# Additive attention rows: the leaky sum in one ScalarE instruction, the mask added by VectorE

## The chip, the cores and the metric

The kernel runs on one core of a Trainium2 chip. The metric is the device time of one execution in microseconds; times of several executions are given as their median. A core has TensorE (PE; its weight loads are PEld), VectorE (DVE), ScalarE (ACT) and GpSimd (POOL), which run their own instruction streams and meet only at semaphores, and SyncE (SP), which here issues the DMAs.

## The reference

Four layers over a batch of 8 graphs with 2048 nodes and 64 features; after each, the input is added and a layer norm follows. Layer 0 is a gated neighbour sum. Layer 1 is dot-product attention with four heads and a second dot-product attention over their output. Layers 2 and 3 are attention with additive scores:

```
e   = left[:, :, None] + right[:, None, :]
e   = where(e >= 0, e, slope * e)            # slope 0.01 in layer 2, 0.2 in layer 3
att = softmax(where(mask, e, -inf))          # mask = adjacency; layer 2 also opens the diagonal
out = att @ h
```

## The kernel before, in words

The first 0.25 ms or so are layer 0 for all batches. The rest (`attention_layers`) is cut into rows: a row is 128 nodes of one attention unit against all 2048 nodes, so a unit has 16 rows. A batch has seven units: four heads (units 0 to 3), the second dot-product attention (unit 4, `GAT2`), and the two additive layers (unit 5, `ADD1`; unit 6, `ADD2`). The order of rows is written out by hand in `loop_order`: after a prologue come seven turns of a loop, and in each turn pairs of additive rows alternate with pairs of head rows of the next batch (first the 16 rows of `ADD1`, later the 16 of `ADD2`). In the last turn only three pairs of `ADD2` have head rows between them and the other ten rows follow each other. The epilogue has the last batch's unit 4, `ADD1` and `ADD2`, one unit after the other, with nothing between.

Every engine walks through the same steps, one row a step, in program order. For a dot-product row TensorE writes the scores of step s into `pss`, four banks of PSUM that hold one row. For an additive row ScalarE writes `pss` from SBUF (`lift_row`, L1283), a step ahead, in two halves. VectorE then reads each half (`masked_scores`, L1392), adds a second operand, takes the row's extremum and writes `rows`, a ring of four rows in SBUF. ScalarE takes the exponential in place (L1301). Two steps later TensorE turns the row in four tiles of 4 blocks (L1102) through `ring`, three banks of PSUM; a tile is copied to `pt` by ScalarE (L1253) or VectorE (L1404): of a dot-product row two tiles each, of an additive row one by ScalarE and three by VectorE. Then TensorE multiplies by the values (`po`, L1129), a pair of rows at a time.

The second operand of L1392 is the mask (bf16, SBUF) for a dot-product row. For an additive row it is a row that GpSimd has put into `rows` beforehand (`mask_row`): slope times the right terms (`sr`) plus the mask (L925), and in `ADD2` also a 128x128 block `shut` that closes the diagonal where the adjacency has no self edge (L922, L929). What ScalarE lifts is the rest of the leaky sum, a ReLU with scale (1-slope)/slope. GpSimd makes the masked row one step ahead, as soon as the ring's place is free.

Beside the rows each engine has tasks hung on steps. VectorE's that matter here: `bend_block` (L1411, leaky ReLU of 256 columns of `zt`, in place), the low halves of projections (L1355, two instructions), the layer norms (L1375, L317, L319, L326, L328). GpSimd's: scaling finished pairs (`finish`, L938 to L951) and the layer norms' powers and products (L894 to L908). The projection tile `hc` is turned by TensorE at L1061, the input of an additive layer at L1032.

Of the kernel before, what the change touches and what calls it, by code (L numbers as in the profile page):

```python
# [34 lines left out]
P = 128  # L35
# [645 lines left out]
def attention_layers(nc, x1, out, whd, bh, wod, bo, gamma, beta, w2, a2, w3, a3,  # L681
# [3 lines left out]
    with ctx:  # L685
# [22 lines left out]
        shut = sb("shut", [P, P], BF16)  # L708
# [47 lines left out]
        mr_ready = sem("mr_ready")  # L756
# [119 lines left out]
        def _(pool):  # L876
# [4 lines left out]
            sr_c = Count(sr_ready)  # L881
            tr_c = Count(tr_ready)
            mr_c = Count(mr_ready)
# [4 lines left out]
            def run_task(name, unit, c):  # L888
# [18 lines left out]
                elif name in ("ld", "rb"):  # L907
                    nc.gpsimd.tensor_tensor(xbc, xbc, spread(rstd, CH), ALU.mult)\  # L908
                      .then_inc(x_done if unit == ADD2 else x_ready, 1)
                elif name == "r":  # L910
                    sr_c.n += 1
# [3 lines left out]

            def mask_row(row):

                if row.t == 0:
                    wait(sr_c)
                if row.unit == ADD2:  # L920
                    drain_link(pool)
                    nc.gpsimd.tensor_tensor(shut[:], ident[:], shut_by[:, row.t:row.t + 1].to_broadcast([P, P]),  # L922
                                            ALU.mult)
                wait(tr_c, tr_c.n + NC * (row.slot_user + 1))
                masked = nc.gpsimd.tensor_tensor(rows[:, row.slot, :], sr[:], mask[:, row.t, :], ALU.add)  # L925
                if row.unit == ADD2:
                    drain_link(pool)
                    own = rows[:, row.slot, row.t * P:(row.t + 1) * P]
                    masked = nc.gpsimd.tensor_tensor(own, own, shut[:], ALU.add)  # L929
                masked.then_inc(mr_ready, 1)  # L930
# [23 lines left out]
            def run_segment(segment):  # L954
                for s in segment.steps:
                    row = segment.row(s + 1)
                    if row and not row.gat and row.t > 0:
                        mask_row(row)
# [4 lines left out]

                    if row and not row.gat and row.t == 0:
                        mask_row(row)
                copied_c.n += segment.pairs
                rc_c.n += segment.pairs
                tr_c.n += NC * segment.blocks
                mr_c.n += segment.adds
# [204 lines left out]
        def _(act):  # L1174
# [28 lines left out]
            def run_task(name, unit, c):  # L1203
# [26 lines left out]
                elif name == "h":  # L1230
# [3 lines left out]
                    nc.scalar.mul(ls[:, unit - ADD1, blocks].unsqueeze(2), pair[:, :, D:D + 1], 1.0 - SLOPES[unit])  # L1234
                    nc.scalar.copy(rt[:, blocks].unsqueeze(2), pair[:, :, D + 1:D + 2]).then_inc(lr_ready, 1)
                    nc.scalar.copy(hn[hn_of(unit)][:, blocks, :], pair[:, :, 0:D]).then_inc(hn_ready, 1)
                elif name == "r":
                    next_of(right_c)
                    sr_c.n += 1
                    nc.scalar.mul(sr[:, cols], px[:], SLOPES[unit]).then_inc(sr_ready, 1)  # L1240
# [33 lines left out]
            def lift_row(row, half):  # L1274

                slope = SLOPES[row.unit]
# [237 lines left out]
```

## Time and profile before

| | |
|---|---|
| median of three runs | 5698.53 us (5693.42 to 5699.99) |
| the profiled execution | 5694.06 us, span of the trace 5692.3 us |
| mean granted TensorE clock | 0.973 of full |
| busy: TensorE / VectorE / ScalarE / GpSimd | 93% / 78% / 65% / 34% of the span |
| instructions of the span | 131823 |

Busy shares are means over stretches of different kinds; a turn of the loop takes about 666 us, of which the two stretches with additive rows take about 166 and 176 us.

### The profile page before, as it was taken

Reading aid. Unit: us, or ns where it says so; the run is one execution under the profiler, and the core shown is the slowest. Engines: PE = TensorE matmul, PEld = TensorE weight load, DVE = VectorE, ACT = ScalarE, POOL = GpSimd, SP = SyncE. Lnnn points to the kernel's source line nnn. Section 1 sums busy time; section 2 is a strip of 40 time slices with the busy share of each in tenths; the row PEclk is TensorE's granted clock in tenths of the full one; section 3 lists DMA queues with packets and bytes.
Section 4 is the critical chain, followed back from the end, with each engine's and each line's share of the span. In section 5 each row is a group of like instructions: output and inputs, shape, how many; then the busy total and the mean of one; then the engine's idle time right before and its main releaser. Section 6 shows DMA issues by size and latency. Waiting matters only on the chain.

```text
span 5692.3 us, 131823 instructions
## 1 busy us (share of the span) xinstructions
PE 5277.2 (93%) x52866; PEld 4523.5 (79%) x52866; DVE 4418.0 (78%) x7321; ACT 3722.7 (65%) x5489; POOL 1940.8 (34%) x1724
## 2 busy tenths in 40 slices
PE   8499999999999899999999999998999999999866
PEld 6388888878878788787888888787887878888755
DVE  5677678787787778877787877877788777877766
ACT  3266567675676757776576766767577766767665
POOL 4300024251243413333242522425133332424366
PEclk9799999999999999999999999999999999999988
DMA  5200000000000000000000000000000000000000
GB/s 177 61 16 11 18 9 9 9 11 18 9 13 7 13 14 13 13 7 15 15 9 9 11 18 9 13 5 14 15 13 12 7 15 14 9 9 5 13 1 5
DMA packets 135486, 94.35 MB, mean 17 GB/s; under 512 B 93792, under 2 KB 112864, under 8 KB 134880
## 3 DMA queue, kind: packets, MB, share of 16 engines
q1 hardware_dynamic: 134880, 85.92, 6.0%
q8 instruction: 423, 6.93, 0.5%
q14 instruction: 183, 1.50, 0.1%
HBM read 35.03 MB, written 8.91 MB: 8 GB/s over the span
## 4 chain that ended last, share of the span: by engine, by line
PE 75%; DVE 8%; issue 5%; ACT 4%; DVEq 2%; POOLq 1%; DMA 0%; SPq 0%; POOL 0%; ACTq 0%
PE po L1129 24%; PE ring L1102 24%; PE pss L1093 10%; PE pss L1094 10%; DVE rows L1392 3%; DVE pt L1404 3%; PE ring L1051 2%; ACT rows L1301 2%; PE ring L1117 2%; DVEq L311 2%; POOLq L311 1%; ACT pss L1283 1%; PE ring L1068 1%; DVE ha L1355 1%; PE ring L1061 1%
## 5 line engine op out<-in xcount | busy, mean ns | idle before, releaser
L1102 PE MATMUL ring<-ident,rows 128*128 128x128 f32 x14336 | 1942.0, 278 | 137.3 <-DVE pt L1404 85.0
L1301 ACT ACTIVATE rows<-rows,nm 128x2048 f32<-128x2048 f32 x896 | 1794.6, 2003 | 315.3 <-DVE nm L1392 310.4
L1404 DVE COPY pt<-ring 128x512 f32<-128x512 f32 x2048 | 1330.4, 685 | 840.4 <-PE ring L1102 834.0
L1102 PEld LDWEIGHTS ring<-ident,rows 128*128 128x128 f32 x14336 | 1606.1, 142 | 373.5 <-issue 204.5
L1129 PE MATMUL po<-pt,hn 128*64 128x128 f32 x28672 | 1776.8, 277 | 35.0 <-ACT zt L1260 22.5
L1129 PEld LDWEIGHTS po<-pt,hn 128*64 128x64 f32 x28672 | 1562.6, 138 | 190.2 <-issue 166.8
L1253 ACT COPY pt<-ring 128x512 f32<-128x512 f32 x1536 | 837.2, 588 | 771.8 <-PE ring L1102 761.5
L925 POOL TENSOR_TENSOR rows<-sr,mask 128x2048 f32<-128x2048 f32 x256 | 1052.2, 4112 | 416.9 <-PE ring L1102 410.6
L1093 PE MATMUL pss<-ha 128*128 128x512 f32 x2560 | 1068.7, 417 | 39.3 <-DMA ha<-hb 38.1
L1094 PE MATMUL pss<-ha,hb 128*128 128x512 f32 x2560 | 1015.1, 397 | 0.0
L1392 DVE CUSTOM_DVE_ANT_0 rows<-pss,mask,nm 128x1024 f32<-128x1024 f32 x640 | 821.5, 1284 | 89.3 <-issue 3.4
L1392 DVE CUSTOM_DVE_ANT_0 rows<-pss,mask 128x1024 f32<-128x1024 f32 x640 | 772.8, 1208 | 86.4 <-PE pss L1094 48.5
L938 POOL TENSOR_TENSOR zt<-zt,ob 128x128 f32<-128x128 f32 x256 | 117.5, 459 | 1786.0 <-ACT ob L1271 1786.0
L1283 ACT ACTIVATE pss<-sr,ls 128x1024 f32<-128x1024 f32 x512 | 563.6, 1120 | 71.5 <-DVE nm L1392 69.5
L1093 PEld LDWEIGHTS pss<-ha 128*128 128x128 f32 x2560 | 486.4, 190 | 127.6 <-DMA ha<-hb 40.5
L1094 PEld LDWEIGHTS pss<-ha,hb 128*128 128x128 f32 x2560 | 487.6, 190 | 86.9
L1392 DVE CUSTOM_DVE_ANT_0 rows<-pss,rows,nm 128x1024 f32<-128x1024 f32 x256 | 328.6, 1284 | 34.8 <-issue 1.0
L894 POOL TENSOR_TENSOR st<-st,half_power 128x4 f32<-128x4 f32 x128 | 131.6, 1028 | 656.4 <-DVE st L330 656.4
L1392 DVE CUSTOM_DVE_ANT_0 rows<-pss,rows 128x1024 f32<-128x1024 f32 x256 | 305.2, 1192 | 38.9 <-POOL rows L929 23.6
L1423 DVE RECIPROCAL rcw<-rs 128x128 f32<-128x128 f32 x256 | 241.5, 943 | 1.2
L940 POOL TENSOR_SCALAR zt<-zt,bhs 128x128 f32<-128x128 f32 x256 | 154.8, 605 | 44.0 <-issue 44.0
L1219 ACT COPY hc<-ring 128x512 f32<-128x512 f32 x80 | 46.9, 586 | 185.7 <-PE ring L1051 185.7
(109 smaller groups left out, 3291.2 us busy)
## 6 DMA issues: line engine op xcount, KB each, us to landing
hb<-ha SPq DMA_DIRECT2D x160, 128.0 KB, 2.3
ha<-hb SPq DMA_DIRECT2D x160, 128.0 KB, 2.3
adjb<-in_adj SPq DMA_DIRECT2D x32, 512.0 KB, 5.5
xb<-in_x SPq DMA_DIRECT2D x16, 256.0 KB, 2.9
x<-t SPq DMA_DIRECT2D x16, 256.0 KB, 2.4
xin<-x SPq DMA_DIRECT2D x32, 128.0 KB, 2.5
xb<-x SPq DMA_DIRECT2D x8, 512.0 KB, 3.9
out<-xb SPq DMA_DIRECT2D x32, 128.0 KB, 2.1
```

What stands on the lines that cost most here:

```text
L311: eng.drain()
L925: masked = nc.gpsimd.tensor_tensor(rows[:, row.slot, :], sr[:], mask[:, row.t, :], ALU.add)
L1093: nc.tensor.matmul(pss[:, cols], ha[i][:, rows_t], moving, start=True, stop=False)
L1094: last = nc.tensor.matmul(pss[:, cols], hb[i][:, rows_t], moving, start=False, stop=True)
L1102: last = nc.tensor.transpose(tile[:, r * P:(r + 1) * P], rows[:, row.slot, jb * P:(jb + 1) * P], ident[:])
L1129: last = nc.tensor.matmul(po[side * D:(side + 1) * D, 0:P], hn[row.hn][:, r, :], pt[:, r, first + side, :], start=(r == 0), stop=(r == NB ...
L1253: nc.scalar.copy(pt[:, CH * q:CH * (q + 1), row.k % SLOTS, :], tile_of("turn", row.k, q)[:].rearrange("p (j n) -> p j n", n=P)).then_inc(p ...
L1283: nc.scalar.activation(pss[:, cols], sr[:, cols], ACT.Relu, scale=(1.0 - slope) / slope, bias=ls[:, row.unit - ADD1, row.t:row.t + 1]).the ...
L1301: nc.scalar.activation(rows[:, row.slot, :], rows[:, row.slot, :], ACT.Exp, scale=-1.0, bias=nm[:, row.place, 1:2], accum_out=rs[:, row.pl ...
L1392: nc.vector.tensor_tensor_reduce(out=scores, in0=pss[:, cols], in1=mask[:, row.t, cols] if row.gat else scores, scale=-1.0, scalar=(-2 * M ...
L1404: nc.vector.tensor_copy(pt[:, CH * q:CH * (q + 1), row.k % SLOTS, :], tile_of("turn", row.k, q)[:].rearrange("p (j n) -> p j n", n=P)).the ...
L1423: nc.vector.reciprocal(rcw[:].rearrange("p (r n) -> p r n", r=2), rs[:, pair].unsqueeze(2).to_broadcast([P, 2, D])).then_inc(rc_ready, 1)
```

## The change

ScalarE's `lift_row` becomes one parametric ReLU with the slope as its `alpha`, on right term plus left bias, so that `pss` holds the whole leaky sum; the small copies of left and right terms lose their factors. `masked_scores` adds the mask itself for every kind of row. For an `ADD2` row VectorE first adds the diagonal block into `pss` in a `scalar_tensor_tensor` of 128 columns in the half where the block lies. GpSimd's `mask_row`, its tile `shut` and the semaphore `mr_ready` go away; VectorE waits in its place for the ring's place to be free, as dot-product rows do.

```diff
@@ gpsimd
-            def mask_row(row):
-                if row.t == 0:
-                    wait(sr_c)
-                if row.unit == ADD2:
-                    drain_link(pool)
-                    nc.gpsimd.tensor_tensor(shut[:], ident[:], shut_by[:, row.t:row.t + 1].to_broadcast([P, P]),
-                                            ALU.mult)
-                wait(tr_c, tr_c.n + NC * (row.slot_user + 1))
-                masked = nc.gpsimd.tensor_tensor(rows[:, row.slot, :], sr[:], mask[:, row.t, :], ALU.add)
-                if row.unit == ADD2:
-                    drain_link(pool)
-                    own = rows[:, row.slot, row.t * P:(row.t + 1) * P]
-                    masked = nc.gpsimd.tensor_tensor(own, own, shut[:], ALU.add)
-                masked.then_inc(mr_ready, 1)
@@ scalar, tasks "h" and "r"
-                    nc.scalar.mul(ls[:, unit - ADD1, blocks].unsqueeze(2), pair[:, :, D:D + 1], 1.0 - SLOPES[unit])
+                    nc.scalar.copy(ls[:, unit - ADD1, blocks].unsqueeze(2), pair[:, :, D:D + 1])
-                    nc.scalar.mul(sr[:, cols], px[:], SLOPES[unit]).then_inc(sr_ready, 1)
+                    nc.scalar.copy(sr[:, cols], px[:]).then_inc(sr_ready, 1)
@@ scalar, lift_row
-                nc.scalar.activation(pss[:, cols], sr[:, cols], ACT.Relu, scale=(1.0 - slope) / slope,
-                                     bias=ls[:, row.unit - ADD1, row.t:row.t + 1]).then_inc(lift_ready, 1)
+                nc.scalar.activation(pss[:, cols], sr[:, cols], ACT.Prelu, scale=1.0,
+                                     bias=ls[:, row.unit - ADD1, row.t:row.t + 1],
+                                     alpha=SLOPES[row.unit]).then_inc(lift_ready, 1)
@@ vector, masked_scores
                 if half == 0:
-                    if not row.gat:
-                        wait(mr_c, mr_c.n + row.nth + 1)
-                    elif row.slot_user >= 0 or tr_c.n:
+                    if row.slot_user >= 0 or tr_c.n:
                         wait(tr_c, tr_c.n + NC * (row.slot_user + 1))
                 else:
                     drain_link(dve)
                 count = scores_c if row.gat else lift_c
                 wait(count, count.n + 2 * row.nth + half + 1)
+                if row.unit == ADD2 and row.t * P // HALF == half:
+                    own = pss[:, row.t * P:(row.t + 1) * P]
+                    nc.vector.scalar_tensor_tensor(out=own, in0=ident[:], scalar=shut_by[:, row.t:row.t + 1],
+                                                   in1=own, op0=ALU.mult, op1=ALU.add)
+                    drain_link(dve)
                 nc.vector.tensor_tensor_reduce(
-                    out=scores, in0=pss[:, cols], in1=mask[:, row.t, cols] if row.gat else scores,
+                    out=scores, in0=pss[:, cols], in1=mask[:, row.t, cols],
```

## Rows read from the trace of the kernel before

**Rows 1.** The page: busy us and share of each engine, instructions.
```profile
PE 5277.2 (93%) x52866; PEld 4523.5 (79%) x52866; DVE 4418.0 (78%) x7321; ACT 3722.7 (65%) x5489; POOL 1940.8 (34%) x1724
```

**Rows 2.** First turn's additive stretches: us, PE, PEld, DVE, ACT, POOL busy; clock.
```profile
887.00:1053.00 166.00, 153.97 (x1629) 130.80 (x1627) 145.02 (x234) 130.01 (x182) 75.91 (x44) 0.98 0.05 11
...
1144.00:1320.00 176.00, 160.52 (x1691) 137.20 (x1691) 142.56 (x233) 130.31 (x182) 88.22 (x72) 0.97 0.05 12
```

**Rows 3.** Groups of instructions, GpSimd: count, busy us, mean ns, idle before.
```profile
L925 POOL TENSOR_TENSOR rows<-sr,mask 128x2048 f32<-128x2048 f32 x256 | 1052.2, 4112 | 416.9 <-PE ring L1102 410.6 <-ACT sr L1240 6.1
```

**Rows 4.** VectorE: two groups with their means; three lines with min/median/max ns.
```profile
L1411 DVE SCALAR_TENSOR_TENSOR zt<-zt 128x256 f32<-128x256 f32 x128 | 105.2, 822 | 0.0
L1355 DVE TENSOR_TENSOR ha<-hc,hb 64x512 fp32r<-64x512 f32 x80 | 79.8, 997 | 1.1
...
L1411 DVE SCALAR_TENSOR_TENSOR zt<-zt x128: 411/421/2864, 323.0 to 5286.6; 128x256 f32<-128x256 f32 x128
...
L1355 DVE TENSOR_TENSOR ha<-hc,hb x80: 689/690/4458, 253.0 to 5305.7; 64x512 fp32r<-64x512 f32 x80
...
L319 DVE SCALAR_TENSOR_TENSOR xb<-st,xb x96: 424/425/4053, 775.6 to 5686.5; 128x256 f32<-128x256 f32 x96
```

**Rows 5.** Timeline near 1015 us: start, duration, engine, line.
```profile
1015.26 4.40 POOL L925 TENSOR_TENSOR rows<-sr,mask 128x2048 f32<-128x2048 f32 x1 [0.41 <-PE ring L1102]
1015.75 4.46 DVE L1355 TENSOR_TENSOR ha<-hc,hb 64x512 fp32r<-64x512 f32 x1
...
1020.98 1.12 PE L1061 MATMUL ring<-ident,hc 128*128 128x128 f32 x4 [5.81 <-DVE pt L1404]
1021.89 1.91 PE L1102 MATMUL ring<-ident,rows 128*128 128x128 f32 x8
```

**Rows 6.** Timeline near 1274 us, VectorE and TensorE.
```profile
1273.78 2.46 DVE L1411 SCALAR_TENSOR_TENSOR zt<-zt 128x256 f32<-128x256 f32 x1
...
1276.89 1.33 PE L1051 MATMUL ring<-zt,wo 64*64 64x128 f32 x10 [2.32 <-DVE pt L1404]
```

**Rows 7.** Durations by line, min/median/max ns: the lift, a table load, additive L1392.
```profile
L1283 ACT ACTIVATE pss<-sr,ls x512: 1097/1119/1162, 883.1 to 5659.3; 128x1024 f32<-128x1024 f32 x171
...
L580 ACT ACT_TABLE_LOAD  x1: 1283/1283/1283, 0.7 to 0.7; - x1
...
L1392 DVE CUSTOM_DVE_ANT_0 rows<-pss,rows x256: 1152/1212/1227, 887.2 to 5661.7; 128x1024 f32<-128x1024 f32 x128
L1392 DVE CUSTOM_DVE_ANT_0 rows<-pss,rows,nm x256: 1282/1284/1286, 888.5 to 5663.1; 128x1024 f32<-128x1024 f32 x128
```

**Rows 8.** Timeline of a mixed `ADD2` pair in the first turn.
```profile
1166.43 2.17 PE L1102 MATMUL ring<-ident,rows 128*128 128x128 f32 x16
...
1167.19 1.29 DVE L1404 COPY pt<-ring 128x512 f32<-128x512 f32 x2
...
1171.57 1.29 DVE L1404 COPY pt<-ring 128x512 f32<-128x512 f32 x2 [0.53 <-PE ring L1102]
```

**Rows 9.** Timeline of the epilogue: `ADD1` starts and runs, then `ADD2` starts.
```profile
5449.81 2.15 ACT L1283 ACTIVATE pss<-sr,ls 128x1024 f32<-128x1024 f32 x2
...
5453.89 1.22 DVE L1392 CUSTOM_DVE_ANT_0 rows<-pss,rows 128x1024 f32<-128x1024 f32 x1 [12.03 <-POOL rows L925]
...
5455.26 1.28 DVE L1392 CUSTOM_DVE_ANT_0 rows<-pss,rows,nm 128x1024 f32<-128x1024 f32 x1
...
5466.34 1.21 DVE L1392 CUSTOM_DVE_ANT_0 rows<-pss,rows 128x1024 f32<-128x1024 f32 x1
...
5470.69 1.22 DVE L1392 CUSTOM_DVE_ANT_0 rows<-pss,rows 128x1024 f32<-128x1024 f32 x1
...
5573.55 2.15 ACT L1283 ACTIVATE pss<-sr,ls 128x1024 f32<-128x1024 f32 x2
...
5578.65 1.22 DVE L1392 CUSTOM_DVE_ANT_0 rows<-pss,rows 128x1024 f32<-128x1024 f32 x1 [13.04 <-POOL rows L929]
...
5583.81 1.23 DVE L1392 CUSTOM_DVE_ANT_0 rows<-pss,rows 128x1024 f32<-128x1024 f32 x1 [2.50 <-POOL rows L929]
```

More of the change, by code:

```diff
@@ L707, in attention_layers @@
         ob = sb("ob", [P, 2, D], F32)
-        shut = sb("shut", [P, P], BF16)
         nm = sb("nm", [P, NB, 2], F32)
@@ L755, in attention_layers @@
         lift_ready = sem("lift_ready")
-        mr_ready = sem("mr_ready")
         scores_read = sem("scores_read")
@@ L880, in _ @@
             rc_c = Count(rc_ready)
-            sr_c = Count(sr_ready)
-            tr_c = Count(tr_ready)
-            mr_c = Count(mr_ready)
             def wait(count, n=None):
@@ L909, in run_task @@
                       .then_inc(x_done if unit == ADD2 else x_ready, 1)
-                elif name == "r":
-                    sr_c.n += 1
             def each(v):
                 return v[:].unsqueeze(1).to_broadcast([P, CH, D])
-            def mask_row(row):
-                if row.t == 0:
-                    wait(sr_c)
-                if row.unit == ADD2:
-                    drain_link(pool)
-                    nc.gpsimd.tensor_tensor(shut[:], ident[:], shut_by[:, row.t:row.t + 1].to_broadcast([P, P]),
-                                            ALU.mult)
-                wait(tr_c, tr_c.n + NC * (row.slot_user + 1))
-                masked = nc.gpsimd.tensor_tensor(rows[:, row.slot, :], sr[:], mask[:, row.t, :], ALU.add)
-                if row.unit == ADD2:
-                    drain_link(pool)
-                    own = rows[:, row.slot, row.t * P:(row.t + 1) * P]
-                    masked = nc.gpsimd.tensor_tensor(own, own, shut[:], ALU.add)
-                masked.then_inc(mr_ready, 1)
             def finish(row):
@@ L955, in run_segment @@
                 for s in segment.steps:
-                    row = segment.row(s + 1)
-                    if row and not row.gat and row.t > 0:
-                        mask_row(row)
                     if segment.finished(s):
@@ L962, in run_segment @@
                         run_task(*task)
-                    if row and not row.gat and row.t == 0:
-                        mask_row(row)
                 copied_c.n += segment.pairs
                 rc_c.n += segment.pairs
-                tr_c.n += NC * segment.blocks
-                mr_c.n += segment.adds
             run_segments(run_segment)
@@ L1274, in lift_row @@
             def lift_row(row, half):
-                slope = SLOPES[row.unit]
                 cols = slice(half * HALF, (half + 1) * HALF)
@@ L1326, in _ @@
             lift_c = Count(lift_ready)
-            mr_c = Count(mr_ready)
             tr_c = Count(tr_ready)
@@ L1449, in run_segment @@
                 lift_c.n += 2 * segment.adds
-                mr_c.n += segment.adds
                 drain_link(dve)
```

## The prediction

> **What bounds the kernel now.** I read the page first: TensorE is busy 93% of the span and VectorE 78% [rows 1], and the chain that ended last is made of TensorE's matmuls for the most part. So TensorE is the bound, and a change that touches only the other three engines can move the time only where TensorE stands still. Next I read the stretches. Where additive rows alternate with head rows, TensorE is idle 12.0 of 166 us (`ADD1`) and 15.5 of 176 us (`ADD2`), with VectorE busy 87% and 81% and GpSimd 46% and 50% [rows 2]. That is where the changed work lies, seven times over. The groups show what GpSimd does there: 256 instructions of 4.1 us, 1052 us in all [rows 3]. The table of waits has almost no wait of VectorE for them in the loop, so at first sight they cost nothing.
>
> The durations by line say otherwise. L1411 takes 421 ns in the median and 2864 at most; L1355 690 and up to 4458; L319 425 and up to 4053 [rows 4]. All have two inputs in SBUF. The timeline shows where the long ones lie: an L1355 of 4.46 us began 0.49 us after an L925 and ended at 1020.21, 0.55 us after that L925 (1019.66) [rows 5]. VectorE was counted as busy, but was held for the length of GpSimd's instruction. L1392 with one input in PSUM never shows this (1282 to 1286 ns in 256 instructions, half of all additive halves) [rows 7]. What the reader is to see in [rows 5, 6] is who pays: VectorE's copy of a turned tile stands behind the held instruction, the bank of `ring` comes free late, and TensorE waits 5.81 and 2.32 us.
>
> **The change part by part.**
>
> *The masked rows go (gain in the loop).* Held time is mean less median, times the count: L1411 128 x (822 - 421) = 51.3 us, L1355 80 x (997 - 690) = 24.6 us, together 76 us [rows 4]. All of L1411 and L1355 lies ahead of the epilogue's additive rows. The other form of L1355 is held a little too; I set it against the few that end behind GpSimd's short instructions, which stay. How much of it does TensorE feel? L1411 held for 2.04 us (2.46 - 0.42) gave a wait of 2.32 us, and L1355 held for 3.77 us, with an L1411 shortly before, one of 5.81 us [rows 5, 6]. TensorE waits for such copies now and then where nothing is held, so some of it would be waited anyway. I take 0.9: 68 us. The bounds are 0.5 and 1.
>
> After the wait of 5.81 us TensorE's clock is low: 8 transposes took 1.91 us, where 16 take 2.17 us at full clock, and the four ahead of them 1.12 us against 0.54 by the same rate [rows 5, 8]. So the wait costs another 0.83 + 0.58 = 1.4 us. It comes once in each of the seven turns, and less than 1 us of wait should be left in its place, as after the shorter waits, which show no slow matmul: 7 x 1.4 = 10 us. Bounds 0 and 10.
>
> The page SBUF — State Buffer of the Trainium skill (section Who interferes with whom) has the mechanism as a rule: a VectorE instruction with two SBUF inputs and a GpSimd instruction that reads SBUF exclude each other for a whole instruction, and with at most one SBUF input VectorE is not held. The trace agrees, with 4.46 us against 0.69 us. By the rule the new block instruction, with `ident` in SBUF and `pss` in PSUM, would not be held either; no row here shows that form.
>
> *The diagonal block moves to VectorE (cost).* 128 new instructions of 128 columns. From L1411's 411 ns at 256 columns and L1392's 1212 ns at 1024, a column costs 1.04 ns, which gives 411 - 133 = 278 ns. A per-partition scalar adds at most what `nm` adds to L1392, 1284 - 1212 = 72 ns, so 0.28 to 0.35 us [rows 4, 7]. The drain before the next instruction costs 0.15 us, as between the halves of L1392 (the first ends at 5455.11, the second begins at 5455.26) [rows 9]. I take 0.47 us each, with bounds 0.28 and 0.6. That is 60 us of VectorE in all. In a mixed pair the first of them stands ahead of the copies at 1167.19. TensorE turned four tiles from 1166.43 in 2.17 us with three banks: the fourth began about 1168.0, and the first copy ended about 1167.8 [rows 8]. So there is 0.2 us of slack, and 0.47 us late makes TensorE 0.3 us late here. The second adds another 0.47 us, but there VectorE waited 0.53 us for TensorE anyway [rows 8], and it waits again in the two head rows behind. Other pairs carry VectorE tasks as well, so I take 0.4 us a pair. Six turns have 8 mixed pairs, the last one 3: 51 x 0.4 = 20 us. Bounds 0, and 51 x 0.94 = 48 us.
>
> *The lift (no cost).* Same instruction, operands and columns: 1119 ns, with a spread of 65 ns [rows 7]. What the function and its `alpha` add is not in the trace. ScalarE ran copies, ReLUs, squares and exponentials after one single table load, so functions shared a table. I take 0; below nothing is excluded by the same columns, above stands the rival below. The copies without a factor are the same ScalarE instructions; 0.
>
> *The wait.* VectorE now waits for the ring's place where it waited for GpSimd. GpSimd waited for the same turns first and then took 4.1 us, so the new wait ends earlier in all cases. Queued behind it are the other half, the copies and tasks.
>
> *Epilogue (gain).* `ADD1` began its first L1392 4.08 us after its lift began, held by L925; with the first half lifted in 1.1 us it can begin 2.9 us sooner. For `ADD2` the distance is 5.10 us against 1.1 + 0.47, so 3.5 us [rows 9]. Then `ADD2` ran a row in 5.16 us, each waiting for GpSimd (5583.81 less 5578.65), and `ADD1` in 4.35 us on VectorE (5470.69 less 5466.34) [rows 9]. With the block that is 4.82, so 0.34 us a row over 15 rows, 5 us. One L319 was held 3.6 us there [rows 4]; I give 3 of it. In all 14 us, bounds 8 and 20. The ten rows at the end of the last turn run at GpSimd's pace too: 8 x 0.34 = 3 us.
>
> *Sum* against the profiled execution of 5694.06 us: -68 - 10 + 20 - 14 - 3 = -75, so 5619. The median of the runs shown is 4.5 us above that execution; for a median I forecast 5623 us.
>
> **The rivals.**
>
> *VectorE takes back more.* VectorE is busy 87% in the first mixed stretch as it is [rows 2], and the order of rows is tight. If every block instruction passes whole (48 us in the loop) and only half of the held time was felt (38 us, no clock gain), the sum is -38 + 48 - 17 = -7; with one of the two alone it is -47 (-68 - 10 + 48 - 17) or -35 (-38 + 20 - 17). With both it would be no change that can be told; the case stands for one of them. For it: 0.2 us of slack in [rows 8]. Against it: VectorE waits for TensorE several times in each group of four rows. Time 5650 to 5685.
>
> *Slower: the parametric ReLU is in another table than the exponential.* Place: between L1283 and L1301 on ScalarE. Each additive row would need two loads, 256 x 2 x 1.283 = 657 us of ScalarE [rows 7]. ScalarE is idle 36 of 166 us in the mixed stretch [rows 2], and 32 loads there are 41 us, so it would become the bound, and most loads lie ahead of an exponential that TensorE waits for. At half of them felt: 5623 + 330 = 5950. It decides once more than 75 of the 657 us pass. Against it: the single load of the trace, though that covers only the functions used. The page ScalarE: Activation LUTs of the Trainium skill (section Table sets: the hidden batching unit) says that cheap functions are in every set, but does not list this one, and puts a switch at about 2.66 us with its drain; by that figure the 512 would be an estimated 1360 us. The trace has 1.283 us for the load alone.
>
> *Not felt.* The held instructions cost VectorE time that it would have waited for TensorE anyway, and the gains of the epilogue are eaten by the block: within 11 us of before. Against it stand the two waits of TensorE in [rows 5, 6].
>
> **How the numbers follow.** Forecast (5592 to 5650): 0.68. VectorE takes back more (5650 to 5687): 0.17. More than I count, from GpSimd's other work coming sooner and waits that vanish whole (below 5592; with every bound on its good side -76 - 10 - 0 - 20 - 3 = -109, 5590): 0.06. Not felt: 0.04. Another table: 0.05. What a measurement of this kernel can tell from no change is about 0.2%, 11 us. Faster 0.68 + 0.17 + 0.06 = 0.91, same 0.04, slower 0.05. The range 5592 to 5668 leaves out 0.06 below, and above it 0.09 and about a quarter of the second case, 0.2 in all.
>
> **What the profile after would show.** Right: L1411 and L1355 with maxima below 1 us; TensorE's wait near 1021 us below 1 us and no slow transposes after it; the first mixed stretch some 8 us shorter than 166, the second about even (4 us less held, 3 more of block); L1283 at 1.12 us and one table load; 128 new VectorE instructions of about 0.33 us; the epilogue's first `ADD1` scores 1.2 us after the lift begins; `ADD2` rows at 4.8 us. Wrong: held instructions still there behind L894 to L951; TensorE's waits for L1404 in the `ADD2` stretch growing by more than 0.5 us a pair; table loads between lift and exponential.

## The result and the profile after

The changed kernel takes 5621.3 us in the median of four runs (5620.65 to 5622.09), the kernel before 5698.6 us (5693.42 to 5699.99): a ratio of 0.9866 with a 95% interval of 0.9849 to 0.9883, so 77 us less. The forecast was 5623 us with a range of 5592 to 5668.

The page of the profile after, first the busy time and instructions of each engine, then of its groups those that answer to [rows 1] and to the two waits that matter below (busy us, mean ns, idle time before and its releaser):

```profile
PE 5261.1 (94%) x52866; PEld 4501.0 (80%) x52866; DVE 4372.5 (78%) x7449; ACT 3722.1 (66%) x5489; POOL 775.2 (14%) x1212
...
L1071 PE MATMUL ring<-ident,rows 128*128 128x128 f32 x14336 | 1939.5, 278 | 114.6 <-DVE pt L1375 79.9
...
L1098 PE MATMUL po<-pt,hn 128*64 128x128 f32 x28672 | 1770.9, 276 | 45.3 <-ACT zt L1229 32.5
```

GpSimd has lost 1166 us of busy time. In the loop that alone gives nothing, as VectorE hardly ever waited for it there; it did in the epilogue [rows 9]. VectorE has 45 us less, although it got 128 instructions more and no old one was made cheaper. Its two held lines show why; the view is the durations by line (min/median/max ns), to be read against [rows 4]. L1382 is the old L1411, L1323 the old L1355:

```profile
L1382 DVE SCALAR_TENSOR_TENSOR zt<-zt x128: 411/416/424, 324.3 to 5231.5; 128x256 f32<-128x256 f32 x128
...
L1323 DVE TENSOR_TENSOR ha<-hc,hb x80: 687/689/795, 253.9 to 5246.9; 64x512 fp32r<-64x512 f32 x80
...
L1360 DVE SCALAR_TENSOR_TENSOR pss<-ident,shut_by,pss x128: 271/354/358, 1138.1 to 5590.8; 128x128 f32<-128x128 f32 x128
...
L1251 ACT ACTIVATE pss<-sr,ls x512: 1094/1119/1163, 884.4 to 5587.2; 128x1024 f32<-128x1024 f32 x171
...
L319 DVE SCALAR_TENSOR_TENSOR xb<-st,xb x96: 424/425/427, 776.9 to 5614.5; 128x256 f32<-128x256 f32 x96
...
L580 ACT ACT_TABLE_LOAD  x1: 1283/1283/1283, 0.7 to 0.7; - x1
```

The medians stood still and the maxima fell from 2864, 4458 and 4053 ns to 424, 795 and 427. The lift has the same 1119 ns as a parametric ReLU as it had as a ReLU [rows 7], and there is one table load, so the parametric ReLU needed no load of its own beside the exponential. The block instruction takes 336 ns in the mean.

The place of [rows 5], in the timeline after:

```profile
1014.87 0.69 DVE L1323 TENSOR_TENSOR ha<-hc,hb 64x512 fp32r<-64x512 f32 x1
1015.59 1.29 DVE L1375 COPY pt<-ring 128x512 f32<-128x512 f32 x2
...
1016.34 0.66 PE L1030 MATMUL ring<-ident,hc 128*128 128x128 f32 x4 [0.99 <-DVE pt L1375]
1017.02 1.06 PE L1071 MATMUL ring<-ident,rows 128*128 128x128 f32 x8
```

The low halves take 0.69 us in place of 4.46, TensorE waits 0.99 us in place of 5.81, and the 8 transposes behind it take 1.06 us in place of 1.91. In the stretches of the first turn (us, then PE, PEld, DVE, ACT, POOL busy, clock), which answer to [rows 2]:

```profile
888.50:1047.60 159.10, 152.81 (x1629) 129.73 (x1629) 138.85 (x236) 129.78 (x181) 15.54 (x29) 1.00 0.05 12
1138.50:1313.80 175.30, 160.38 (x1695) 135.47 (x1695) 143.89 (x250) 130.94 (x182) 15.48 (x29) 0.98 0.05 12
```

The first has 7 us less, of them 5.7 us of TensorE's idle time and 1.2 us of its busy time (the slow matmuls); its clock rose from 0.98 to 1.00. The second hardly moved. I measured all stretches of both traces in the same way, from where VectorE starts on the scores of a stretch's first additive row to where it starts on those of the first row behind its last. In the epilogue, too, a unit's part ends with the first scores of the next: how late `ADD1` starts counts to unit 4, and how late `ADD2` starts counts to `ADD1`. In us, summed over the seven turns:

| | before | after | difference |
|---|---|---|---|
| `ADD1` among head rows | 1169.0 | 1114.4 | -54.6 |
| between the two | 633.2 | 636.2 | +3.0 |
| `ADD2` among head rows | 1228.1 | 1220.1 | -8.0 |
| epilogue: unit 4, `ADD1`, `ADD2` | 140.8, 124.8, 113.6 | 137.7, 117.7, 110.6 | -13.2 |

The differences sum to 72.8 us; the two profiled executions, 5694.06 and 5622.09 us, are 72 us apart, the medians 77. Of the 54.6 us, 39.8 are idle time of TensorE and 14.8 its busy time, that is slower matmuls, in all seven turns: the first turn with its 1.2 us has one of the smallest parts.

The epilogue, against [rows 9] (start, duration, engine, line):

```profile
5390.72 2.15 ACT L1251 ACTIVATE pss<-sr,ls 128x1024 f32<-128x1024 f32 x2
...
5391.98 1.23 DVE L1363 CUSTOM_DVE_ANT_0 rows<-pss,mask 128x1024 f32<-128x1024 f32 x1 [9.19 <-ACT pss L1251]
...
5508.02 2.15 ACT L1251 ACTIVATE pss<-sr,ls 128x1024 f32<-128x1024 f32 x2
...
5509.24 0.35 DVE L1360 SCALAR_TENSOR_TENSOR pss<-ident,shut_by,pss 128x128 f32<-128x128 f32 x1 [9.15 <-ACT pss L1251]
5509.71 1.22 DVE L1363 CUSTOM_DVE_ANT_0 rows<-pss,mask 128x1024 f32<-128x1024 f32 x1
...
5517.11 1.22 DVE L1363 CUSTOM_DVE_ANT_0 rows<-pss,mask 128x1024 f32<-128x1024 f32 x1
```

`ADD1` scores 1.26 us after its lift begins, where it took 4.08 us, and `ADD2` 1.69 us where it took 5.10. VectorE's wait there is now for ScalarE.

What is still open is whether the held time is the cause of the gain, what the block costs, and why its gain in `ADD2` is so small. The experiments ask that.

### The profile page after: what moved, and what is told of

It reads as the page before. It is cut to its first block, busy times and chain, and to the rows that moved or that the text cites. A ratio compares the mean times of both kernels' runs of the same rounds, so it can differ in the third digit from the quotient of the medians.

```text
span 5620.3 us, 131303 instructions
## 1 busy us (share of the span) xinstructions
PE 5261.1 (94%) x52866; PEld 4501.0 (80%) x52866; DVE 4372.5 (78%) x7449; ACT 3722.1 (66%) x5489; POOL 775.2 (14%) x1212
## 4 chain that ended last, share of the span: by engine, by line
PE 76%; DVE 8%; issue 5%; ACT 4%; DVEq 2%; DMA 0%; SPq 0%; POOLq 0%; POOL 0%; ACTq 0%
PE po L1098 24%; PE ring L1071 24%; PE pss L1062 10%; PE pss L1063 10%; DVE rows L1363 4%; DVE pt L1375 3%; PE ring L1020 2%; DVEq L311 2%; ACT rows L1270 2%; PE ring L1086 2%; ACT pss L1251 1%; PE ring L1037 1%; ACT pt L1222 1%; PE ring L1030 1%; PE ring L1001 1%
## 5 line engine op out<-in xcount | busy, mean ns | idle before, releaser
L1363 DVE CUSTOM_DVE_ANT_0 rows<-pss,mask,nm 128x1024 f32<-128x1024 f32 x896 | 1150.2, 1284 | 124.1 <-issue 5.8
L1363 DVE CUSTOM_DVE_ANT_0 rows<-pss,mask 128x1024 f32<-128x1024 f32 x896 | 1079.8, 1205 | 105.3 <-PE pss L1063 48.8
L1394 DVE RECIPROCAL rcw<-rs 128x128 f32<-128x128 f32 x256 | 241.6, 944 | 1.2
L924 POOL TENSOR_TENSOR y<-ob,rc 128x128 f32<-128x128 f32 x128 | 51.3, 401 | 1225.1 <-ACT ob L1240 1180.5
L1270 ACT ACTIVATION_READ_ACCUMULATOR rows<-rows,nm 128x1 f32 x896 | 167.8, 187 | 0.0
L1363 DVE DVE_READ_ACCUMULATOR2_ANT nm<- 128x1 f32 x1792 | 148.5, 83 | 0.0
```

Of the source, the lines that this page charges most:

```text
L1270: nc.scalar.activation(rows[:, row.slot, :], rows[:, row.slot, :], ACT.Exp, scale=-1.0, bias=nm[:, row.place, 1:2], accum_out=rs[:, row.pl ...
L1363: nc.vector.tensor_tensor_reduce(out=scores, in0=pss[:, cols], in1=mask[:, row.t, cols], scale=-1.0, scalar=(-2 * MASKED if half == 0 else ...
L1394: nc.vector.reciprocal(rcw[:].rearrange("p (r n) -> p r n", r=2), rs[:, pair].unsqueeze(2).to_broadcast([P, 2, D])).then_inc(rc_ready, 1)
```

## Experiments

Every run was measured against the kernel before on the same chip (medians from 5697.4 to 5699.7 us). "Over the changed kernel" means over 5621.3 us.

### What does the diagonal block cost? noblock and block2

noblock leaves out the closing of `ADD2`'s diagonal (the output lacks just that):

```diff
-                if row.unit == ADD2 and row.t * P // HALF == half:
-                    own = pss[:, row.t * P:(row.t + 1) * P]
-                    nc.vector.scalar_tensor_tensor(out=own, in0=ident[:], scalar=shut_by[:, row.t:row.t + 1],
-                                                   in1=own, op0=ALU.mult, op1=ALU.add)
-                    drain_link(dve)
```

> The kernel after, but the diagonal block instruction of ADD2 (128 of them, VectorE) and its drain are left out, so ADD2's diagonal is not closed where the adjacency has no self edge. Theory of the prediction: 0.4 us a mixed pair x 51 pairs = 20 us in the loop, and up to 0.49 us a row in the 26 additive rows that follow each other (13 us, of which 8 felt): 5621 - 28 = 5593 us (5585 to 5603). Rival 1, every block instruction passes whole: 128 x 0.49 = 63 us, so 5558. Rival 2, all of it hidden in VectorE's waits: 5621 within 4.

Measured: 5599.1 us (5595.1 to 5602.7), ratio 0.9829 (0.9814 to 0.9843). The block costs 22 us. `ADD2`'s seven stretches sum to 1201.9 us without it, 1220.1 with it; of these 18.2 us, 11.5 are idle time of TensorE and 6.6 slower matmuls.

block2 issues the block and its drain twice:

```diff
+                    for _ in range(2):
                         nc.vector.scalar_tensor_tensor(out=own, in0=ident[:], ...)
                         drain_link(dve)
```

> The block instruction and its wait for the pipeline are issued twice at each of the 128 rows of ADD2 that need it (the second adds the shut value to the diagonal once more, so the value is -2 times as low; the output changes by nothing that matters, the diagonal weights are zero either way). Theory A (a pair's cycle in ADD2's mixed stretches passes through VectorE, so the time given to it comes back at about the measured rate of 22 us per block): about 5645, 5640 to 5652, ADD2's mixed stretches 178 to 180. Theory B (the first block eats slack left by the removed hold, the second finds none, so it costs its full 0.35 to 0.47 us x 112 in the loop and x 16 in the epilogue): 5660 to 5680. Theory C (most of the first block's price is its wait for ScalarE's lift, which the second doesn't pay): under 5635.

Measured: 5658.8 us (5654.3 to 5661.4), ratio 0.9932 (0.9915 to 0.9949). The second block costs 37.5 us, 15 more than the first and more than theory A gave; the time lies just short of theory B's interval. `ADD2`'s stretches go to 1247.6 us (+27.5), the epilogue's `ADD2` from 110.6 to 115.8 us. The timeline shows the mechanism. This is a mixed `ADD2` pair of the first turn, in the changed kernel (start, duration, engine, line, and in brackets the idle time before and its releaser):

```profile
1207.64 0.68 DVE L1323 TENSOR_TENSOR hb<-hc,ha 64x512 fp32r<-64x512 f32 x1
1208.02 1.09 PE L1071 MATMUL ring<-ident,rows 128*128 128x128 f32 x8
1208.33 0.69 DVE L1323 TENSOR_TENSOR ha<-hc,hb 64x512 fp32r<-64x512 f32 x1
...
1209.05 1.29 DVE L1375 COPY pt<-ring 128x512 f32<-128x512 f32 x2
...
1209.89 0.83 PE L1071 MATMUL ring<-ident,rows 128*128 128x128 f32 x5 [0.34 <-DVE pt L1375]
```

and the same place in block2:

```profile
1206.28 1.09 PE L1071 MATMUL ring<-ident,rows 128*128 128x128 f32 x8
...
1207.74 1.29 DVE L1376 COPY pt<-ring 128x512 f32<-128x512 f32 x2
...
1208.58 0.94 PE L1071 MATMUL ring<-ident,rows 128*128 128x128 f32 x6 [0.77 <-DVE pt L1376]
```

In noblock TensorE does not stand here, but its matmuls just before were slow (32 in 3.30 us, for 1.97 in the changed kernel), which gave the copies time. The next such place has the same speed in both. The changed kernel waits there, noblock doesn't:

```profile
1233.71 1.16 PE L1071 MATMUL ring<-ident,rows 128*128 128x128 f32 x8 [0.34 <-DVE pt L1375]
```

```profile
1233.97 1.16 PE L1071 MATMUL ring<-ident,rows 128*128 128x128 f32 x8
```

With one block TensorE waits 0.34 us (0.27 and 0.25 us at the like places at 1163 and 1255), with two 0.77 us. So one block with its drain, about 0.47 us, finds some 0.13 us of slack and passes on 0.34; the second finds none and passes on 0.43. That is the step of the prediction that set 0.2 us of slack against 0.47.

### Is it the reading that holds VectorE? ghost, ghostset, ghostlong

These put work back on GpSimd that nobody reads, for the same rows and behind the same waits, into a part of a tile that is not in use. ghost:

```diff
+                wait(tr_c, tr_c.n + NC * (row.slot_user + 1))
+                drain_link(pool)
+                nc.gpsimd.tensor_tensor(by_block(xz[D:P, BANK:N]), ident[D:P, :].unsqueeze(1).to_broadcast([D, 12, P]),
+                                        by_block(mask[D:P, row.t, BANK:N]), ALU.add)
+                drain_link(pool)
```

> The kernel after, with a GpSimd instruction that nobody waits for put back at each additive row, at the step and behind the wait of the old masked row: it adds ident (repeated) and 1536 columns of the mask on 64 partitions into an unused part of xz. An estimate from 4.1 us at 2048 columns is 3.1 us each. Theory A (a GpSimd instruction that reads SBUF and a VectorE instruction with two SBUF inputs exclude each other): held instructions come back with maxima of 3 to 3.5 us, three quarters of the 69 us of the two mixed stretches are lost again: 5621 + 45 to 60 = 5666 to 5681; the starts of ADD1 and ADD2 in the epilogue stay fast. Theory B (the gain came from VectorE and the ring no longer waiting for GpSimd's row): no change against after, 5621 within 5.

Measured: 5629.8 us (5627.6 to 5634.2), 8.5 us over the changed kernel. Both theories' numbers were missed: the instruction was shorter than L925 (3.12 us against 4.11), and so its end fell ahead of the low halves. The timeline near the place of [rows 5]:

```profile
1013.51 3.12 POOL L914 TENSOR_TENSOR xz<-ident,mask 64x1536 f32<-64x1536 f32 x1 [0.16 <-issue]
...
1015.66 0.69 DVE L1390 COPY pt<-ring 128x512 f32<-128x512 f32 x1
1016.26 0.66 DVE L1397 SCALAR_TENSOR_TENSOR zt<-zt 128x256 f32<-128x256 f32 x1
1016.85 0.67 DVE L1338 TENSOR_TENSOR hb<-hc,ha 64x512 fp32r<-64x512 f32 x1
```

The bend began at 1016.26 and ended at 1016.92, 0.29 us behind the end of GpSimd's at 1016.63; the low half behind it was free. In the loop only the bends were held (mean 531 ns, maximum 1141: 14 us in all), and in the epilogue one L319 (3172 ns).

ghostset does the same with instructions that only write:

```diff
+                for _ in range(3):
+                    drain_link(pool)
+                    nc.gpsimd.memset(xz[D:P, BANK:N], 0.0)
+                drain_link(pool)
```

> As ghost, but GpSimd writes SBUF without reading it: three memsets of 1536 columns on 64 partitions at each additive row, an estimated 1.5 us each. Theory A with the rule that only GpSimd's reads collide: nothing held beyond after, 5621 within 5. Theory A in a wider form (any use of SBUF by GpSimd excludes): holds of up to 1.5 us, 5621 + 15 to 40. Theory B: 5621 within 5.

Measured: 5623.6 us (5620.4 to 5627.9), 2.3 us over the changed kernel, whose runs (5620.65 to 5622.09) lie within its own. GpSimd is as busy with them (768 x 1.374 = 1055 us) as with L925 before (1052 us), and no line of VectorE is held:

```profile
L915 POOL MEMSET xz<- x768: 1372/1374/1391, 877.5 to 5584.7; 64x1536 f32 x192
...
L1397 DVE SCALAR_TENSOR_TENSOR zt<-zt x128: 411/417/423, 320.6 to 5230.5; 128x256 f32<-128x256 f32 x128
...
L1338 DVE TENSOR_TENSOR ha<-hc,hb x80: 687/689/799, 250.5 to 5245.9; 64x512 fp32r<-64x512 f32 x80
```

This isn't for want of meetings: 66 bends and 28 low halves began while a memset ran, and none of them took more than 422 and 691 ns. In the kernel before, each of the 42 bends that began during an L925 took 808 ns or more. So it isn't GpSimd's being busy. To have ghost's read at L925's length, ghostlong reads the first input with a stride:

```diff
-                nc.gpsimd.tensor_tensor(by_block(xz[D:P, BANK:N]), ident[D:P, :].unsqueeze(1).to_broadcast([D, 12, P]),
-                                        by_block(mask[D:P, row.t, BANK:N]), ALU.add)
+                nc.gpsimd.tensor_tensor(xz[D:P, BANK:N].rearrange("p (q n) -> p q n", n=32),
+                                        ident[D:P, 0:P:4].unsqueeze(1).to_broadcast([D, 48, 32]),
+                                        mask[D:P, row.t, BANK:N].rearrange("p (q n) -> p q n", n=32), ALU.add)
```

> As ghost, but the first input is read with a stride of 4 elements, which should make GpSimd's instruction longer than the 3.12 us that missed most of VectorE's two-input instructions (in ghost one ended 0.2 us before L1355 began). I guess 4 to 4.8 us. Theory A: the holds come back, as long as GpSimd's instruction lasts, and the time goes up by 0.5 (as in ghost: 8.5 us for 17.5 us held) to 0.9 of the held time: with 30 to 70 us held, 5640 to 5675. Theory B: 5621 to 5632.

Measured: 5700.7 us (5696.9 to 5705.9), ratio 1.0003 (0.9994 to 1.0012). The whole gain is gone, by an instruction whose result nobody waits for. The durations by line, and then the timeline of one turn:

```profile
L914 POOL TENSOR_TENSOR xz<-ident,mask x256: 3776/3906/4231, 884.0 to 5667.1; 64x1536 f32<-64x1536 f32 x128
...
L1398 DVE SCALAR_TENSOR_TENSOR zt<-zt x128: 412/421/1949, 327.1 to 5310.3; 128x256 f32<-128x256 f32 x128
...
L1339 DVE TENSOR_TENSOR ha<-hc,hb x80: 689/689/4198, 256.6 to 5325.7; 64x512 fp32r<-64x512 f32 x80
...
L1376 DVE SCALAR_TENSOR_TENSOR pss<-ident,shut_by,pss x128: 272/354/358, 1148.8 to 5674.4; 128x128 f32<-128x128 f32 x128
```

```profile
1016.15 3.94 POOL L914 TENSOR_TENSOR xz<-ident,mask 64x1536 f32<-64x1536 f32 x1 [0.16 <-issue]
...
1018.90 1.48 DVE L1398 SCALAR_TENSOR_TENSOR zt<-zt 128x256 f32<-128x256 f32 x1
...
1020.57 4.05 POOL L914 TENSOR_TENSOR xz<-ident,mask 64x1536 f32<-64x1536 f32 x1 [0.48 <-PE ring L1087]
1020.99 4.19 DVE L1339 TENSOR_TENSOR ha<-hc,hb 64x512 fp32r<-64x512 f32 x1
...
1025.95 1.12 PE L1046 MATMUL ring<-ident,hc 128*128 128x128 f32 x4 [5.56 <-DVE pt L1391]
```

Each held instruction ends just behind GpSimd's (1020.38 against 1020.09, 1025.18 against 1024.62), and TensorE waits 5.56 us, with the 1.12 us matmuls of [rows 5] behind the wait. The block instruction, one input in PSUM, keeps its 272 to 358 ns, also in the 75 of 128 that began during one of GpSimd's reads. By the Trainium skill (SBUF — State Buffer, section Who interferes with whom) a VectorE instruction with at most one SBUF input, outside its two-port modes, isn't held, and one with two SBUF inputs isn't held by a GpSimd instruction that only writes. L1376 here and the memsets of ghostset agree. So VectorE and GpSimd meet in their reads of SBUF too, and not at semaphores alone, as the section on the cores has it.

The expectation was 5640 to 5675, so more came back than I gave. The held time is 38.5 us (bends) + 24.6 us (low halves) + 3.6 us (L319), 67 us, less than the 85 us of before (51.3 + 24.6 + 5.8 for the other form of L1355 + 3.6), and yet the time went up by 79 us, as much as the change had given. Two things explain most of that.

First, ghostlong has the block and the kernel before doesn't. Like is compared with like when before is set against noblock: there the masked rows cost 5698.6 - 5599.1 = 99 us.

Second, TensorE loses in two ways: it idles, and its matmuls are slower behind some of the waits. The table has both, over the 14 mixed stretches, each kernel against the one that has all its work but GpSimd's reads. "Held" is what bends, low halves and L319 took there over their means in the changed kernel; "busy" is TensorE's busy time:

| | against | held, us | stretches longer, us | TensorE idle more | TensorE busy more |
|---|---|---|---|---|---|
| before | noblock | 76 | 81 | 59 | 22 |
| ghostlong | changed kernel | 60 | 76 | 47 | 29 |
| split (further down) | noblock | 45 | 39 | 33 | 6 |
| add1only (further down) | noblock | 32 | 26 | 20 | 6 |
| ghost | changed kernel | 14 | 5 | 6 | 0 |

The idle time is 0.78, 0.79, 0.73 and 0.63 of the held time, and 0.4 in ghost with its short holds. The rest is the clock. TensorE waited over 2 us for a copy of VectorE 15 times in the loop of before (60.0 us), 7 times in ghostlong (38.8 us), 8 times in split (25.3 us) and never in ghost or the changed kernel. Behind each of the waits of 5.4 to 6.3 us, one a turn in before and ghostlong, the four transposes of [rows 5] took 1.11 or 1.12 us and the eight behind them 1.91; behind a wait of 0.99 us they take 0.66 and 1.06.

### The same reading in shorter pieces: split

The kernel before, with L925 in four instructions of 512 columns:

```diff
-                masked = nc.gpsimd.tensor_tensor(rows[:, row.slot, :], sr[:], mask[:, row.t, :], ALU.add)
+                for c in range(NC):
+                    cols = slice(c * BANK, (c + 1) * BANK)
+                    masked = nc.gpsimd.tensor_tensor(rows[:, row.slot, cols], sr[:, cols], mask[:, row.t, cols],
+                                                     ALU.add)
```

> The kernel before, with the masked row made in four instructions of 512 columns, an estimated 1.1 us each, instead of one of 4.1. Theory A: no VectorE instruction is held longer than about 1.3 us beyond its own time, the 76 us of holding fall to 20 to 30, TensorE's wait of 5.8 us a turn goes; against it GpSimd needs some 0.4 us more a row, which costs 5 to 10 us in the epilogue: 5694 - 40 + 8 = 5662 (5645 to 5675). Theory B: the masked row comes later, not sooner, so 5700 to 5710.

Measured: 5655.8 us (5653.9 to 5658.4), ratio 0.9928 (0.9912 to 0.9945). The four pieces make GpSimd's work 122 us longer (1174.0 against 1052.2 us), and the kernel is 43 us faster. The groups of VectorE (busy us, mean ns):

```profile
L1414 DVE SCALAR_TENSOR_TENSOR zt<-zt 128x256 f32<-128x256 f32 x128 | 83.1, 649 | 0.0
L1358 DVE TENSOR_TENSOR hb<-hc,ha 64x512 fp32r<-64x512 f32 x80 | 68.4, 855 | 12.8 <-ACT hb L1225 12.8
L1358 DVE TENSOR_TENSOR ha<-hc,hb 64x512 fp32r<-64x512 f32 x80 | 68.2, 852 | 1.1
```

A VectorE instruction can now step in between two pieces: the longest low half takes 1648 ns in place of 4458. The held time only falls from 82 to 56 us (128 x (649 - 421) + 80 x (855 - 678) + 80 x (852 - 689) ns), and yet more than half of the change's gain is there. By the table, 31 us less were held in the mixed stretches and TensorE idled 27 us less, 0.86 of it; the other 15 us are faster matmuls. The wait of 5.6 to 6.3 us a turn became one of 3.0 to 3.5, and behind it the four transposes took 0.66 us in all seven turns, the eight behind them 1.06 to 1.10 us in four and 1.63 to 1.94 in three. So cutting the longest holds gave back clock beside the time held. In the epilogue the longer work of GpSimd was felt: `ADD2` took 119.2 us there, for 113.6.

### Which layer gives what? add1only

The kernel before, with `ADD1` done in the new way and `ADD2` in the old:

```diff
-                    if row and not row.gat and row.t > 0:
+                    if row and row.unit == ADD2 and row.t > 0:
                         mask_row(row)
@@ scalar, lift_row
+                if row.unit == ADD1:
+                    nc.scalar.activation(pss[:, cols], sr[:, cols], ACT.Prelu, scale=1.0,
+                                         bias=ls[:, 0, row.t:row.t + 1], alpha=slope).then_inc(lift_ready, 1)
+                    return
@@ vector, masked_scores
-                    out=scores, in0=pss[:, cols], in1=mask[:, row.t, cols] if row.gat else scores,
+                    out=scores, in0=pss[:, cols], in1=scores if row.unit == ADD2 else mask[:, row.t, cols],
```

> The kernel before with ADD1 done in the new way (parametric ReLU, mask by VectorE, no masked row) and ADD2 in the old. By the stretches of the two traces the first mixed stretch gave 54.6 us of the 72, the second 7.6 net and the epilogue 13: this kernel should keep the 54.6 and the epilogue's part up to the end of ADD1, about 9: 5698.5 - 64 = 5635 (5630 to 5642). If instead the gain needs both units (GpSimd wholly free), 5650 or more.

Measured: 5638.7 us (5636.6 to 5640.7), ratio 0.9894 (0.9880 to 0.9907). `ADD1`'s half gives 60 us: its seven mixed stretches sum to 1114.7 us, as in the changed kernel (1114.4), `ADD2`'s to 1228.1, as before. The other half of the change adds 17 us. From noblock, `ADD2`'s stretches would have fallen by 26 us; the block takes 18 of them back.

### Is the bend's own time worth anything? bendbefore and bendafter

L1411 was the line with the most held time. In both kernels I gave it to ScalarE, as a parametric ReLU in place. In bendbefore (and with the same edit in bendafter):

```diff
+            def bend_block(row):
+                part = zt[:, row.unit, (row.t + 1 - CH) // 2:(row.t + 1) // 2, :]
+                wait(out_c, out_c.n + row.pair + 1)
+                nc.scalar.activation(part, part, ACT.Prelu, scale=1.0, alpha=0.2).then_inc(z_ready, 1)
```

> The kernel before, masked rows of GpSimd and all, with L1411 (leaky ReLU of zt, two SBUF inputs on VectorE) done by ScalarE as a parametric ReLU instead. Theory A: the 51 us for which it was held cannot be held any more; L1355's 25 us stay, somewhat shifted; ScalarE gains 128 x 0.4 = 51 us of work, partly felt: 5698.5 - 0.8 x 51 + 10 = 5668 (5655 to 5680). Theory B: GpSimd's rows are as late as before, so only VectorE's 54 us of own work move: 5690 to 5700.

bendbefore measured: 5665.0 us (5664.4 to 5671.0), ratio 0.9942 (0.9929 to 0.9956), 34 us faster than before: theory A. The bend takes 403 to 434 ns on ScalarE, but the low halves are still held (means 1045 and 842 ns), and `ADD1`'s stretches stay at 165 us.

> The changed kernel with the 128 bends of 0.418 us (53.5 us) moved from VectorE to ScalarE. In the kernel before, this move gave 34 us, of which the hold of the bends behind GpSimd (51 us) was the likely part. Theory A (what it gave there was mostly the hold, which is gone now): 5610, 5603 to 5619, most of it in ADD2's mixed stretches, 173 to 174.5 in place of 175.3 to 176.8, and nothing in ADD1's (159). Theory B (the bend's own time on VectorE was what it gave, held or not): 5585 to 5595. Theory C (ScalarE, busy 0.82 in the first mixed stretches, becomes the last to come): 5625 to 5640.

bendafter measured: 5630.1 us (5627.4 to 5631.3), ratio 0.9881 (0.9866 to 0.9896): 9 us slower than the changed kernel. The same move that gave 34 us now costs 9, so what it took away before was the hold and not the bend's own 0.42 us. It is theory C that got the time right, but ScalarE was busy 0.82 of the first mixed stretch without the bends already, and that one didn't get longer: `ADD1`'s stretches sum to 1113.4 us against 1114.4. `ADD2`'s of the first six turns sum to 1058.2 us against 1055.3, and the last turn's alone takes 171.1 us against 164.8. The groups of the page name a new wait, the first line of the changed kernel's page above against this one:

```profile
L1071 PE MATMUL ring<-ident,rows 128*128 128x128 f32 x14336 | 1939.1, 278 | 110.0 <-DVE pt L1384 76.0
...
L1098 PE MATMUL po<-pt,hn 128*64 128x128 f32 x28672 | 1772.3, 277 | 58.8 <-ACT zt L1229 46.9
```

TensorE waits 3.9 us less for VectorE's copies and 14.4 us more for ScalarE's small copy out of `po`, as that now stands behind the bend (bend 1230.51, copy 1230.82, and TensorE's wait for it 1.62 us). As the stretches show, most of these waits cost little in the end. Half of the 9 us lies in one place of the last turn, where TensorE waits for the bend itself, which stands behind an exponential of 1.99 us on ScalarE. First bendafter, then the changed kernel:

```profile
5239.03 6.32 PE L1020 MATMUL ring<-zt,wo 64*64 64x128 f32 x64 [2.47 <-ACT zt L1247]
```

```profile
5232.53 3.71 PE L1020 MATMUL ring<-zt,wo 64*64 64x128 f32 x64 [0.28 <-DVE pt L1375]
```

The wait is 2.2 us longer and the 64 matmuls behind it take 2.6 us more.

### A version that beats both: spread, and spreadbend

VectorE's L1394 takes the reciprocal of two sums, widened to 128 columns: 944 ns, 256 times. In spread it takes it of two columns and GpSimd widens the result with a copy that reads one small column pair:

```diff
+                nc.gpsimd.tensor_copy(rcw[:].rearrange("p (r n) -> p r n", r=2),
+                                      rc[:, pair].unsqueeze(2).to_broadcast([P, 2, D])).then_inc(wide_ready, 1)
@@ vector, invert_sums
-                nc.vector.reciprocal(rcw[:].rearrange("p (r n) -> p r n", r=2),
-                                     rs[:, pair].unsqueeze(2).to_broadcast([P, 2, D])).then_inc(rc_ready, 1)
+                nc.vector.reciprocal(rc[:, pair], rs[:, pair]).then_inc(rc_ready, 1)
```

> The kernel after, with the reciprocal of a head pair's sums taken on 2 columns (0.155 us) in place of 128 (0.944 us), 256 times, and widened by GpSimd, now idle, in a copy of 128 columns that TensorE waits for. VectorE loses 256 x 0.79 = 202 us of work. If VectorE is what TensorE still waits for in the mixed stretches (PE waits for L1375 and L1382's neighbours sum to about 5 us of 15 a turn), 5621 - 7 x 2 to 3 = 5605; if those waits come from the three banks alone, 5621 within 5; if the longer way over GpSimd is late for TensorE, more than 5626.

Measured: 5598.1 us (5594.1 to 5599.7), ratio 0.9822 (0.9808 to 0.9835): 23 us faster than the changed kernel, and the fastest here that computes the whole reference. The groups:

```profile
L917 POOL COPY rcw<-rc 128x128 f32<-128x128 f32 x256 | 74.3, 290 | 2270.4 <-DVE rc L1403 2270.4
L1403 DVE RECIPROCAL rc<-rs 128x2 f32<-128x2 f32 x448 | 69.9, 156 | 1.6
```

VectorE does 201 us less (241.6 + 29.8 against 69.9) and 23 us come of it, 0.11 of it, in the stretches where the head rows stand alone (-7.4 us over the seven between the two kinds, -7.4 over the six between the turns) and in `ADD2`'s (-10.1). GpSimd's new copies are too short, at 0.29 us, to hold anybody for long.

> The changed kernel with both moves: reciprocals on 2 columns and the widening on GpSimd (which alone gave 23 us), and the bend on ScalarE. If both gains come from VectorE's own time in a pair's cycle and add: 5585 to 5592. If the second finds VectorE off the path: 5596 to 5602, as the first alone. If ScalarE becomes the bound: over 5605.

spreadbend has both edits: 5607.7 us (5602.9 to 5608.7), ratio 0.9841 (0.9826 to 0.9856), 9.6 us over spread, the same loss that the bend's move brought to the changed kernel alone. It lies where the third case put it, and as in bendafter ScalarE isn't late throughout: the last turn's `ADD2` stretch takes 170.1 us against 164.3 in spread, with the same wait of 2.47 us for the bend in it.

## Why the prediction was right, step by step

- **The mechanism**, that VectorE is held by GpSimd's reads and TensorE pays, is shown: undone by an unread instruction of the same length the gain is gone (ghostlong), with writes alone it stays (ghostset), with shorter reads more than half of it comes (split).
- **Held time x 0.9, 68 us, and the clock, 10 us.** The loop's mixed stretches without the block fell by 54.6 + 26.2 = 80.8 us (`ADD1` after, `ADD2` in noblock, against before). The two terms and the last turn's 3 us made 81. The parts were less exact, and that they met is luck: TensorE's idle time fell by 59 us, 0.78 of the 76 us held, and its busy time by 22 us. The factor was too high and the clock's term too low, by about the same 12 us. The clock's term counted only the matmuls behind the one long wait a turn (1.4 us), where `ADD1`'s stretches alone lost 1.2 to 3.1 us of busy time a turn. As a law, held time times a factor does for TensorE's idle time where single holds are long (0.73 to 0.79 in before, ghostlong and split); it gives ghost 13 us over the changed kernel where it was 8.5, and the clock has to be added to it.
- **The diagonal block, +20 us in the loop.** Measured +18.2 us in `ADD2`'s stretches, of which 6.6 us are slower matmuls, which the sum didn't have, and +3.0 between the two kinds of stretches, where noblock has none of the 3.0. The instruction took 0.34 us (0.28 to 0.35 predicted), TensorE's wait at the places shown 0.25 to 0.34 us (0.3 predicted for the first block of a pair).
- **The split over the stretches.** Predicted 8 us shorter and about even; measured 7.8 and 1.1 us in the mean of seven turns.
- **The lift, 0.** 1119 ns before and after.
- **Epilogue, -14 us.** Measured -13.2. The starts were right: 2.8 us and 3.4 us sooner for 2.9 and 3.5. With an eye to where a start counts, unit 4's 3.1 us is mostly `ADD1`'s start, and `ADD1`'s 7.1 us is `ADD2`'s start and the 3.6 us of the held L319 (3 predicted). Unit 4's part moves by itself, though: it takes 137.7 us here, 139.7 in noblock and 137.8 in ghostset, with the same code. `ADD2`'s rows gave 3.0 us for 5 predicted: the 4.83 us a row holds only for the first rows (5522.41 to 5527.24); behind the middle, rows take 5.2 to 5.4 us (5549.17, 5554.57, 5559.74, 5565.14), no faster than before.
- **Last turn, -3 us.** Its `ADD2` stretch went from 166.9 to 164.8 us, with its three mixed pairs and the block in it, so this term can't be told apart.
- **Of the rivals**, another table and "not felt" are excluded by the rows and runs above. "VectorE takes back more" was wrong by its size: the block passed 22 us and not 48. The second block of block2, 37.5 us, shows how near it was: of its 60 us (128 x 0.47) 0.62 pass, of the first block's 0.37.

What stays open: why TensorE's matmuls are 12 us slower in ghostlong's `ADD2` stretches than in the changed kernel's, where no wait of over 2 us for VectorE stands; and how much of the "busy" column varies from execution to execution (ghostlong's profiled execution is 5 us over its median, before's 4.5 us under). The 3 us that add up between the two kinds of stretches I found but didn't follow.

## What to carry to other kernels

Look at the maxima of an instruction's duration and not only at its mean. Here the lines whose median stood while the maximum was five times as long or more were held by another engine, and no wait in the profile said so. If VectorE has instructions with two SBUF inputs, either keep GpSimd's reading instructions off those steps, or cut them short; cutting gave more than half of the gain, though it made GpSimd's work 122 us longer, of which some 6 us were felt in the epilogue's `ADD2`. Compare a variant with the kernel that has the same work otherwise: against the changed kernel, which has the block, the cost of the holds looked like 77 us, and it was 99. And an engine's microsecond has no one price: on VectorE it was worth about 0.8 of TensorE's idle time in long holds ahead of the copies, and more with the slower matmuls behind them, 0.4 and then 0.6 in the first and second block ahead of the scores, and 0.1 in the reciprocals.

## What the runs showed of the hardware

- A held VectorE instruction ended a fixed time behind GpSimd's: 0.28 or 0.29 us where it has 256 columns (all 90 bends held by over 0.3 us in before, ghost and ghostlong), and 0.55 us where it has 512 (all 14 low halves in before and ghostlong), less than its own 0.42 and 0.69 us.
- GpSimd's add of 64x1536 took 3.12 us with inputs read in blocks of 128 and 3.91 us with one input in blocks of 32 at a stride of 4; a memset of the same size 1.37 us. The first has half the partitions and three quarters of the columns of L925, and takes 0.76 of its 4.11 us: the columns count here, not the partitions.
- ScalarE's parametric ReLU with bias and `alpha` costs what a ReLU costs, 1119 ns for 1024 columns, and 418 ns in place for 256 columns in SBUF.
